# Two stacked transformer blocks on one core: attention weights loaded head by head, and four FP4 nibbles unpacked in each 16-bit word

## The chip, the core and the metric

The kernel runs on one core of a Trainium2 chip. The metric is device time in microseconds of one execution; each figure of a kernel is the median over several executions. Five engines work side by side and wait for one another through semaphores: PE (the matrix engine), VectorE (DVE in the rows), ScalarE (ACT), GpSimd (POOL) and SyncE (SP), which issues most of the DMA transfers.

## What is computed

Four stages in a row act on x of shape 2 x 512 x 256, each followed by a normalised sum with what went in:

```python
# stage 0: causal attention, 16 heads of 128, with rotary embedding
x = layernorm(h) * ln_g + ln_b
q, k, v = (x @ w.T + b for each);  q, k = rope(q), rope(k)
attn = softmax(mask(q k^T / sqrt(128)));  out = (attn v) @ wo.T + bo + h
# stage 1: MLP 256 -> 2048 -> 256, weights in FP4
low = W_packed & 15;  high = W_packed >> 4 & 15
W = LUT[interleave(low, high)] * scales (one for each block of 32)
out = (gelu(x @ Wg.T) * (x @ Wu.T)) @ Wd.T
# stage 2: linear attention with running sums, 16 heads of 16 (W_qkv, W_out)
# stage 3: MLP 256 -> 688 -> 256, weights by index into a table of 16
```

The packed codes come as int32, one byte of value (0 to 31) in each. All matrix products are made in float16 with a correction: each fp32 operand is split into a high float16 part (`h`) and a low one (`l` = value - h), and three products are added (`product`).

## The kernel before

Tokens are in 8 tiles of 128 rows, four per batch. The order of work on each engine is written out by hand, and nothing is reordered. Attention runs over 32 units (batch b, head h; `UNITS`), in steps `s` from -2 to 33. In step s PE makes the scores of unit s (`scores`), the projection of q and k of unit s+2 in two halves (`project(s + 2, 0)`, `project(s + 2, 1)`, both through the one `proj_bank`), v of unit s (`project_v`), the output projection of unit s-2 (`out_project`) and the weighted sum of unit s-1 (`weigh`). VectorE takes the row maxima (`top`, L977), corrects o (`low_o`, L1013), multiplies each projection half by cosine and sine (`rotate`, L986 and L988), and makes `low_v` (L1007) and the lows of the probabilities (`low_p`, L999). GpSimd adds the rotated halves of unit s+1 (`rotate`, L494 and L495, four ops) and makes the lows of q and k (`low_qk`, L502, two ops). ScalarE makes `exp` (L650), and the high parts (`high_qk` L669, `high_v` L674, `high_p` L661, `high_o` L681). SP turns the probabilities by DMA (`turn`).

The attention weights and those of stage 2 are split on the way. They come in 18 pieces of 128 x 1024 fp32 into a ring of four slots, `stage`. Pieces 0 to 5 hold the first eight heads of wq, wk and wv less their first two heads (768 columns); then follow wo, the other eight heads, the rest of wo, and stage 2's. The first two heads of wq, wk and wv (`EARLY`) come ahead of all in three loads of 256 KB (`early32`), which ScalarE (`high_early`, L611) and VectorE (`low_early`, L916) split. `LOWS_AT` names the step of each piece: in it ScalarE makes the high part (`high_w`, L625), for GpSimd's pieces it also scales the staged values (L627), and then either GpSimd (`low_w`, L472, `ALL_POOL_W`) or VectorE (`prepare`, L936, `DVE_LOWS`: every second piece from 6 on) makes the whole low. SP's `load_w(j + 4)` waits until the low of piece j has freed its slot. GpSimd's `rotate(u)` waits for its own lows before it.

Batch 0 is normalised and turned by PE before the steps (`turn_norm0`, `turned_x0` L923, `high_xT0` L621, `low_xT0` L929). Batch 1 is turned in steps 4 and 5 (`X0_TURN_AT`), one half each, through `proj_bank`: at the step's end PE waits for VectorE's second `rotate(s + 2, 1)`, transposes four tiles (L1337), and `turned_x0` comes behind that rotation. ScalarE normalises four tiles each in steps 2, 7 and 9 (`X0_NORM_AT`). GpSimd adds a bias row to four tiles in steps 10 and 12 (`residual`, L479).

FP4: 12 pieces of 512 columns. `unpacked(j)` and `signed(j)` on VectorE make from 512 int32 words two tiles of FP8 bit patterns and their sign bits, in five ops (L962 to L971). GpSimd multiplies each by the scales (`scaled`, L521, reading one byte in four), ScalarE and VectorE split the product (`high_fp4` L719, `low_fp4` L1114). Pieces 0 to 2 are unpacked around the end of attention, pieces 3 to 11 beside the first tiles of the first of two MLP passes (`unpack_beside`); there each tile of 128 hidden values goes through gelu (L737), `product_of` (L1162), its high part (L743) and low part on GpSimd (`low_inter`, L525), and PE's `gate_up` and `down`.

Of the kernel before, what the change touches and what calls it, by code (L numbers as in the profile page):

```python
# [79 lines left out]
def sandwich(nc, x_in, wqT, wkT, wvT, woT, bqT, bkT, bvT, bo, gT, bT, ropes, w1T, packed, scales, codes, lut, out):  # L80
    with ExitStack() as ctx:
# [3 lines left out]
        def sem(name):  # L85
# [34 lines left out]
        wh = [sb(f"w{n}h", [P, 4096], F16) for n in "qkvo"]  # L120
        wl = [sb(f"w{n}l", [P, 4096], F16) for n in "qkvo"]
# [12 lines left out]
        sign = xT[:, 0, :].bitcast(I32)  # L134
# [31 lines left out]
        early32 = pT[:, :, :, :, :].rearrange("p w k i n -> p (w k i n)").bitcast(F32)[:, 0:3 * KC * EARLY].rearrange(  # L166
            "p (w c n) -> p w c n", w=3, c=KC)
# [8 lines left out]
        bits = [prob[:, 0, 2 * i:2 * i + 2, :].bitcast(I32) for i in range(NIBBLES)]  # L176
# [13 lines left out]
        fh = [w[:, :].rearrange("p (c n) -> p c n", c=NIBBLES) for w in wh[0:3]]  # L190
        fl = [w[:, :].rearrange("p (c n) -> p c n", c=NIBBLES) for w in wl[0:3]]
# [13 lines left out]
        d_bits = sem("d_bits")  # L205
        a_fh = sem("a_fh")
# [83 lines left out]
        w_dram = [w.rearrange("(c p) n -> p c n", p=P) for w in (wqT, wkT, wvT, woT)]  # L290

        def w_piece(j):

            return W_ORDER[j]

        def w_cols(j):

# [77 lines left out]
        def _(sp):  # L375
# [1321 lines left out]
```

## Time and profile before

| | us |
|---|---|
| median of 3 runs (702.53 to 702.62) | 702.58 |
| the profiled execution | 699.39 |
| its span in the profile | 697.6 |

| engine | busy us | share of the span |
|---|---|---|
| PE | 561.1 | 80% |
| VectorE | 549.6 | 79% |
| ScalarE | 399.6 | 57% |
| GpSimd | 388.6 | 56% |

The mean granted PE clock of the span is 0.93 of full. The span is what the profiler saw of one execution from the first to the last instruction; a little time lies around it. A share of busy time is a mean over stages that have different limits, so the rows below are taken by stage. In a row of the timeline stand the start, the time until its end (of all instructions merged in the row), the engine, the line of the kernel, the operation, what is written and read, the shapes and, in brackets, how long the engine was idle before and what it waited for. Names such as `turned`, `rr` or `pT` are buffers that serve several purposes in turn.

### The profile page before, as it was taken

What the parts mean: (1) busy time and instruction counts of PE and PEld (TensorE: products, weight loads), DVE (VectorE), ACT (ScalarE), POOL (GpSimd) and SP (SyncE); (2) the same over time, 40 slices, a digit from 0 to 9 for tenths busy, and PEclk for the clock granted to TensorE, in tenths of its full rate; (3) what the DMA queues carried; (4) which work ended last, traced back from release to release, by engine and by line L of the source; (5) the groups of instructions that cost most, each with busy time, mean ns of one, the idle gap of its engine ahead of it and who ended that gap; (6) DMA issues with size and microseconds to landing.
All of it is one profiled execution on the core that took longest, in us unless ns stands there. A gap on an engine that the chain in (4) does not pass through costs nothing.

```text
span 697.6 us, 10855 instructions
## 1 busy us (share of the span) xinstructions
PE 561.1 (80%) x3843; PEld 339.9 (49%) x3848; DVE 549.6 (79%) x1103; ACT 399.6 (57%) x838; POOL 388.6 (56%) x312
## 2 busy tenths in 40 slices
PE   5378788989899999999777787969964968793494
PEld 2145456565566666666543444535532634352252
DVE  6578779878789998998799999887469494667643
ACT  4578667877776687787744344355542345462141
POOL 3698866999988787778456566211442101154021
PEclk8899989999999999999989999989989899997597
DMA  7255443433335485344332130111001010000000
GB/s 257 83 129 126 105 110 81 95 77 68 52 76 74 77 179 90 66 66 75 78 101 76 62 90 1 32 39 34 1 0 46 15 32 1 0 1 0 0 31 30
DMA packets 100741, 44.58 MB, mean 64 GB/s; under 512 B 88272, under 2 KB 93520, under 8 KB 100688
## 3 DMA queue, kind: packets, MB, share of 16 engines
q1 hardware_dynamic: 99696, 43.35, 28.1%
q8 instruction: 30, 0.49, 0.3%
q10 hardware_dynamic: 992, 0.55, 0.3%
q14 instruction: 23, 0.19, 0.1%
HBM read 21.86 MB, written 1.05 MB: 33 GB/s over the span
## 4 chain that ended last, share of the span: by engine, by line
PE 39%; DVE 29%; issue 10%; ACT 9%; POOL 6%; POOLq 0%; DVEq 0%; ACTq 0%
PE bank L1325 34%; PE bank L1501 3%; DVE turned L1153 2%; DVE stage L1182 2%; DVE turned L1162 2%; DVE stats L849 2%; POOL rr L494 1%; POOL rr L495 1%; DVE xT L964 1%; DVE pT L962 1%; DVE y L863 1%; DVE pT L963 1%; DVE pT L971 1%; DVE wql L1114 1%; DVE wkl L1114 1%
## 5 line engine op out<-in xcount | busy, mean ns | idle before, releaser
L525 POOL TENSOR_TENSOR qkl<-turned,qkh 128x512 f16<-128x512 f32 (+1 forms) x44 | 57.4, 1304 | 178.3 <-ACT qkh L743 178.3
L494 POOL TENSOR_TENSOR rr<-turned 64x512 f32<-64x512 f32 x64 | 86.7, 1354 | 12.2 <-DVE turned L988 8.2
L502 POOL TENSOR_TENSOR qkl<-rr,qkh 128x512 f16<-128x512 f32 x64 | 73.8, 1158 | 29.4 <-ACT qkh L669 27.0
L743 ACT ACTIVATE qkh<-turned 128x512 f16<-128x512 f32 (+1 forms) x44 | 27.7, 629 | 108.5 <-DVE turned L1162 108.5
L650 ACT ACTIVATE bank<-bank,nmax 128x128 f32<-128x128 f32 (+3 forms) x128 | 64.1, 501 | 37.8 <-DVE nmax L977 37.3
L495 POOL TENSOR_TENSOR rr<-turned 64x512 f32<-64x512 f32 x64 | 81.9, 1279 | 3.7
L977 DVE TENSOR_REDUCE nmax<-bank 128x1 f32<-128x128 f32 (+3 forms) x128 | 58.2, 484 | 15.0 <-PE bank L1371 13.3
L1162 DVE SCALAR_TENSOR_TENSOR turned<-bank,turned 128x512 f32<-128x512 f32 (+1 forms) x44 | 30.0, 682 | 46.4 <-PE bank L1325 20.8
L999 DVE SCALAR_TENSOR_TENSOR parts<-bank,rscaled,parts 128x128 f16<-128x128 f32 (+3 forms) x128 | 65.8, 547 | 0.3 <-ACT parts L661 0.3
L1325 PE MATMUL bank<-qkh 128*128 128x128 f16 (+3 forms) x128 | 38.9, 304 | 24.7 <-issue 16.3
L661 ACT ACTIVATE parts<-bank,rscaled 128x128 f16<-128x128 f32 (+3 forms) x128 | 57.2, 529 | 1.2 <-DMA pT<-parts 0.2
L1325 PE MATMUL bank<-pT,vh 128*128 128x512 f16 (+3 forms) x256 | 56.6, 311 | 1.5 <-DVE vl L1007 1.2
L1325 PE MATMUL bank<-xTh,wkh 128*128 128x512 f16 x128 | 50.1, 391 | 5.6 <-DVE turned L988 4.4
L1325 PE MATMUL bank<-xTh,wqh 128*128 128x512 f16 x128 | 50.5, 395 | 1.5 <-DVE turned L988 1.5
L1325 PE MATMUL bank<-xTl,wqh 128*128 128x512 f16 x128 | 50.1, 392 | 0.0
L1325 PE MATMUL bank<-xTh,wql 128*128 128x512 f16 x128 | 50.0, 391 | 0.0
L669 ACT ACTIVATE qkh<-rr 128x512 f16<-128x512 f32 x64 | 40.5, 634 | 16.1 <-POOL rr L495 16.1
L1325 PE MATMUL bank<-xTl,wkh 128*128 128x512 f16 x128 | 49.8, 389 | 0.0
L1325 PE MATMUL bank<-xTh,wkl 128*128 128x512 f16 x128 | 49.7, 388 | 0.0
L1325 PE MATMUL bank<-wvh,qkh 128*128 128x256 f16 x128 | 36.3, 284 | 16.3 <-POOL qkl L525 16.3
L1325 PE MATMUL bank<-wvh,xTh 128*128 128x128 f16 x256 | 44.6, 219 | 2.2 <-DVE ol L1013 2.2
L1325 PE MATMUL bank<-wvh,xTl 128*128 128x128 f16 x256 | 44.5, 219 | 0.0
(224 smaller groups left out, 1722.4 us busy)
## 6 DMA issues: line engine op xcount, KB each, us to landing
xa<-in_codes SPq DMA_DIRECT2D x32, 128.0 KB, 2.7
stage<-in_packed SPq DMA_DIRECT2D x12, 256.0 KB, 3.1
stage<-in_scales SPq DMA_DIRECT2D x12, 256.0 KB, 3.7
stage<-in_woT SPq DMA_DIRECT2D x4, 512.0 KB, 3.5
pT<-parts SPq DMA_TRANSPOSE x128, 2.8
x<-in_x SPq DMA_DIRECT2D x2, 512.0 KB, 7.2
stage<-in_wqT SPq DMA_DIRECT2D x2, 512.0 KB, 4.2
stage<-in_wkT SPq DMA_DIRECT2D x2, 512.0 KB, 4.0
```

The lines of the kernel that those rows point to most:

```text
L494: pool.tensor_tensor(rr[low, w, :], cos_a[part], sin_b[part], ALU.subtract)
L495: pool.tensor_tensor(rr[high, w, :], cos_b[part], sin_a[part], ALU.add).then_inc(g_rot, 1)
L502: pool.tensor_tensor(qkl[:, p, w, :], rr[:, w, :], qkh[:, p, w, :], ALU.subtract).then_inc(g_qkl, 1)
L525: pool.tensor_tensor(il[n % 2][0:rows, :], inter[0:rows, n % 2, :], ih[n % 2][0:rows, :], ALU.subtract).then_inc(g_il, 1)
L650: act.activation(row, row, ACT.Exp, bias=nmax[:, p, q:q + 1], accum_out=psum_row[:, p, q:q + 1]).then_inc(a_exp, 1)
L661: act.activation(row_parts[q][:, :, 0, :], row_bank[q][:, 0:(q + 1) * P].rearrange("p (k n) -> p k n", n=P), ACT.Copy, scale=rscaled[:, p, ...
L669: act.activation(qkh[:, p, w, :], rr[:, w, :], ACT.Copy).then_inc(a_qkh, 1)
L743: act.activation(ih[n % 2][0:rows, :], inter[0:rows, n % 2, :], ACT.Copy).then_inc(a_ih, 1)
L977: dve.tensor_reduce(nmax[:, p, q:q + 1], row_bank[q][:, 0:(q + 1) * P], AX_X, ALU.max, negate=True).then_inc(d_max, 1)
L999: dve.scalar_tensor_tensor(out=row_parts[q][:, :, 1, :], in0=row_bank[q][:, 0:(q + 1) * P].rearrange("p (k n) -> p k n", n=P), scalar=rsca ...
L1162: dve.scalar_tensor_tensor(out=inter[0:rows, n % 2, :], in0=U_bank[n % 2][0:rows, :], scalar=1 / (X_SCALE * W_SCALE), in1=gel[0:rows, n % ...
L1325: last = pe.matmul(dst, l, r, start=start and i == 0, stop=stop and i == 2, skip_group_check=skip)
```

## The change

- Weights by head. The host packs q, k, v and o of each head side by side; a piece is now one head (256 columns each of q, k, v, o), 16 pieces and two for stage 2. The early loads and their splits are gone. One piece falls in each step from -1 to 14, piece 1 in step -2, and piece 0 before the steps.
- Lows shared. Of each head's piece GpSimd makes the low of the first 768 columns, VectorE that of the last 256 (`POOL_COLS`); piece 0 is wholly VectorE's, stage 2's two are GpSimd's. ScalarE makes the highs one step ahead.
- Batch 1's transposes in mid-step. PE makes them after `project_v`, waiting for the first rotation half only; VectorE's `turned_x0` stands ahead of `low_p`.
- FP4. ScalarE copies each int32 piece to bytes (`to_bytes`); VectorE works on 256 uint16 words, each holding two bytes, so four nibbles.

```diff
-LOWS_AT = {-2: (0, 1, 2, 3), -1: (4, 5), 0: (6,), 1: (7,), ... 9: (15,), 11: (16,), 13: (17,)}
-DVE_LOWS = (6, 8, 10, 12, 14, 16)
+W_PIECES = HEADS + 2
+LOWS_AT = {-2: (1,), **{s: (s + 3,) for s in range(-1, HEADS - 1)}}
+POOL_COLS = 3 * D
+BYTES_AT = tuple(range(UNITS - 6, UNITS - 2))
...
+byte = xT[:, 0, :].bitcast(U8).rearrange("p (i n) -> p i n", n=Q_COLS)
-bits = [prob[:, 0, 2 * i:2 * i + 2, :].bitcast(I32) for i in range(NIBBLES)]
+bits = [prob[:, 0, i, :].bitcast(U8).rearrange("p (e n) -> p e n", n=Q_COLS) for i in range(NIBBLES)]
...
+def of_head(h, w, c=0):
+    o = w * D + c * DK
+    n = D if w == 3 else DK
+    return [a[:, h, o:o + n] for a in (w_all_h, w_all_l)]
 def lows_before(j):
-    g = sum(i in ALL_POOL_W for i in range(j))
-    return j - g, g
+    return min(j, HEADS), max(j - 1, 0)
... SP
-for w in range(3):
-    sp.dma_start(early32[:, w, :, :], w_dram[w][:, :, 0:EARLY]).then_inc(s_early[w], 16)
 def load_w(j):
     if j >= 4:
         by_dve, by_pool = lows_before(j - 3)
+        if by_pool:
+            sp.wait_ge(g_wl, by_pool)
+        sp.wait_ge(d_wl, by_dve)
+    src = per_head[j] if j < HEADS else w1_dram[:, j - HEADS, :]
+    sp.dma_start(stage[:, j % 4, :], src).then_inc(s_w[j % 4], 16)
... GpSimd
 def low_w(j):
     pool.wait_ge(a_wh, j + 1)
+    n = POOL_COLS if j < HEADS else W_COLS
+    pool.tensor_tensor(w_low(j)[:, 0:n], stage[:, j % 4, 0:n], w_high(j)[:, 0:n], ALU.subtract).then_inc(g_wl, 1)
-code = bits[j % 2][:, c, :].bitcast(FP8).rearrange("p (n e) -> p n e", e=4)[:, :, 0]
+code = bits[j % 2][:, c, :].bitcast(FP8)
... ScalarE
 def high_w(j):
     act.wait_ge(s_w[j % 4], 16 * (j // 4 + 1))
+    n = POOL_COLS if 0 < j < HEADS else W_COLS
+    for cols in (slice(0, n), slice(n, W_COLS))[:1 if n == W_COLS else 2]:
+        last = act.activation(w_high(j)[:, cols], stage[:, j % 4, cols], ACT.Copy, scale=W_SCALE)
+    if j:
+        last = act.activation(stage[:, j % 4, 0:n], stage[:, j % 4, 0:n], ACT.Copy, scale=W_SCALE)
     last.then_inc(a_wh, 1)
 in step(s):
-    for j in LOWS_AT.get(s, ()):
-        if j >= 2:
-            high_w(j)
+    for j in LOWS_AT.get(s + 1, ()):
+        high_w(j)
+def to_bytes(j):
+    act.wait_ge(s_raw[j % 4], 32 * (j // 4 + 1))
+    if j >= 4:
+        act.wait_ge(d_bits, 2 * (j - 3))
+    act.activation(byte[:, j % 4, :], raw[:, j % 4, :], ACT.Copy).then_inc(a_byte, 1)
+# called behind steps 26 to 29 for pieces 0 to 3, and one MLP tile ahead of unpacked(j) for 4 to 11
... VectorE
+def low_w(j):
+    cols = slice(POOL_COLS if j else 0, W_COLS)
+    dve.wait_ge(a_wh, j + 1)
+    dve.scalar_tensor_tensor(out=w_low(j)[:, cols], in0=stage[:, j % 4, cols], scalar=W_SCALE,
+                             in1=w_high(j)[:, cols], op0=ALU.mult, op1=ALU.subtract).then_inc(d_wl, 1)
 def prepare(s):          # last in step(s), behind rotate(s + 2, 1)
     for j in LOWS_AT.get(s, ()):
+        if j < HEADS:
+            low_w(j)
 def unpacked(j):
-    dve.tensor_scalar(low, r, 2, 0x1C, ALU.logical_shift_left, ALU.bitwise_and)
-    dve.tensor_scalar(high, r, 2, 0x1C, ALU.logical_shift_right, ALU.bitwise_and)
-    dve.tensor_scalar(sign, r, 4, 0x80, ALU.logical_shift_left, ALU.bitwise_and).then_inc(d_bits, 1)
+    r = byte[:, j % 4, :].bitcast(U16)
+    low, high, sign = (bits[j % 2][:, i, :].bitcast(U16) for i in range(3))
+    dve.wait_ge(a_byte, j + 1)
+    dve.tensor_scalar(low, r, 2, 0x1C1C, ALU.logical_shift_left, ALU.bitwise_and)
+    dve.tensor_scalar(sign, r, 4, 0x8080, ALU.logical_shift_left, ALU.bitwise_and)
+    dve.tensor_scalar(high, r, 2, 0x1C1C, ALU.logical_shift_right, ALU.bitwise_and).then_inc(d_bits, 1)
 in step(s):
     if there(s):
         inverse(s)
         low_v(s)
+    if s in X0_TURN_AT:
+        turned_x0(1, (X0_TURN_AT[s],))
+    if there(s):
         for q in range(TPB):
             low_p(s, q)
     if there(s + 2):
         rotate(s + 2, 1)
-    if s in X0_TURN_AT:
-        turned_x0(1, (X0_TURN_AT[s],))
... PE, in step(s)
     if there(s):
         project_v(s)
+    if s in X0_TURN_AT:
+        pe.wait_ge(d_rope, 2 * (s + 2) + 1)
+        turn_norm0(1, (X0_TURN_AT[s],))
...
     if there(s + 2):
         project(s + 2, 1)
-    if s in X0_TURN_AT:
-        pe.wait_ge(d_rope, 2 * (s + 2) + 2)
-        turn_norm0(1, (X0_TURN_AT[s],))
```

## Rows read from the trace of the kernel before

**Rows 1.** Busy time by stage: PE, PEld, DVE, ACT, POOL; granted clock; DMA share, GB/s.

```profile
34.00:202.00 168.00, 145.48 (x1195) 95.61 (x1196) 135.50 (x249) 126.41 (x305) 145.15 (x113) 0.97 0.44 92
202.00:346.00 144.00, 137.20 (x1184) 93.03 (x1184) 127.76 (x258) 110.39 (x284) 111.25 (x90) 1.00 0.50 88
346.00:435.00 89.00, 66.40 (x355) 36.96 (x355) 88.38 (x134) 37.41 (x60) 52.44 (x36) 0.90 0.23 67
```

**Rows 2.** Timeline of the opening, all engines: start, us.

```profile
6.79 0.61 ACT L611 ACTIVATE wqh<-pT 128x512 f16<-128x512 f32 x1
...
8.43 0.69 DVE L916 SCALAR_TENSOR_TENSOR wql<-pT,wqh 128x512 f16<-128x512 f32 x1
...
10.94 0.84 ACT L625 ACTIVATE wqh<-stage 128x768 f16<-128x768 f32 x1 [0.97 <-DMA stage<-in_wqT]
...
12.42 1.13 ACT L621 ACTIVATE xTh<-xT 128x512 f16<-128x512 f32 x2
...
13.07 2.31 DVE L929 TENSOR_TENSOR xTl<-xT,xTh 128x512 f16<-128x512 f32 x2 [1.40 <-ACT xTh L621]
...
15.44 1.03 PE L1463 MATMUL bank<-zerob,identb 128*128 128x512 bf16 x2 [4.91 <-DVE xTl L929]
...
19.16 0.75 DVE L986 SCALAR_TENSOR_TENSOR turned<-bank,bias_q,rope 128x512 f32<-128x512 f32 x1
...
23.71 2.47 DVE L910 SCALAR_TENSOR_TENSOR shift<-mv,rstd 128x4 f32<-128x4 f32 x3
```

**Rows 3.** Timeline, two of GpSimd and the first scores on PE.

```profile
22.92 3.24 POOL L472 TENSOR_TENSOR wkl<-stage,wkh 128x768 f16<-128x768 f32 x2 [6.04 <-ACT stage L627]
...
34.04 0.26 PE L1325 MATMUL bank<-qkh 128*128 128x128 f16 x1 [5.01 <-POOL qkl L502]
...
37.26 1.26 POOL L494 TENSOR_TENSOR rr<-turned 64x512 f32<-64x512 f32 x1 [0.17 <-POOL wvl L472]
```

**Rows 4.** Timeline of GpSimd in the steps, and the scores of unit 16.

```profile
45.09 2.17 POOL L494 TENSOR_TENSOR rr<-turned 64x512 f32<-64x512 f32 x1 [0.22 <-DVE turned L988]
...
54.65 2.13 POOL L472 TENSOR_TENSOR wol<-stage,woh 128x1024 f16<-128x1024 f32 x1 [0.73 <-ACT stage L627]
...
76.94 1.27 POOL L494 TENSOR_TENSOR rr<-turned 64x512 f32<-64x512 f32 x1 [0.17 <-POOL wql L472]
...
82.27 2.27 POOL L502 TENSOR_TENSOR qkl<-rr,qkh 128x512 f16<-128x512 f32 x2
...
151.76 2.78 POOL L479 TENSOR_TENSOR xa<-xa,bo_row 128x256 f32<-128x256 f32 x4
...
192.55 1.26 POOL L494 TENSOR_TENSOR rr<-turned 64x512 f32<-64x512 f32 x1 [0.22 <-DVE turned L988]
...
201.48 0.22 PE L1325 MATMUL bank<-qkh 128*128 128x128 f16 x1 [0.17 <-issue]
```

**Rows 5.** Timeline of VectorE's weight lows and of batch 1's first transposes.

```profile
44.93 1.22 DVE L936 SCALAR_TENSOR_TENSOR wol<-stage,woh 128x1024 f16<-128x1024 f32 x1
...
84.74 1.12 PE L1337 MATMUL bank<-identf,nrm 128*128 128x128 f32 x4 [3.47 <-DVE turned L988]
...
86.62 1.80 DVE L936 SCALAR_TENSOR_TENSOR wkl<-stage,wkh 128x1024 f16<-128x1024 f32 x1
```

**Rows 6.** VectorE's busy time in stretches that hold one unpacking each.

```profile
358.97:361.30 2.33, 2.30 (x7) 0.56 0.54 171
...
370.15:375.22 5.07, 5.04 (x6) 0.95 0.27 73
...
390.30:393.47 3.17, 3.14 (x6) 1.00 0.02 5
...
sum 44.94, DVE 44.53; mean DVE 3.71
```

**Rows 7.** One op of an unpacking (timeline), and four f16 ops (chain).

```profile
391.42 1.52 DVE L970 TENSOR_TENSOR pT<-pT,xT 128x512 int32<-128x512 int32 x1
...
450.08 1.05 DVE rope L1153 x4
```

More of the change, by code:

```diff
@@ L13 @@
 I32 = mybir.dt.int32
+U16 = mybir.dt.uint16
+U8 = mybir.dt.uint8
 P = 128
@@ L77, with sandwich @@
 TURNS = ((0, 0), (0, 1), (1, 0), (1, 1), (2, 0), (3, 0), (2, 1), (3, 1))
-def sandwich(nc, x_in, wqT, wkT, wvT, woT, bqT, bkT, bvT, bo, gT, bT, ropes, w1T, packed, scales, codes, lut, out):
+def sandwich(nc, x_in, per_head, bqT, bkT, bvT, bo, gT, bT, ropes, w1T, packed, scales, codes, lut, out):
     with ExitStack() as ctx:
@@ L488, in rotate @@
                     pool.wait_ge(g_qkl, 2 * u)
-                pieces = [j for k in range(-2, u - 1) for j in LOWS_AT.get(k, ()) if j in ALL_POOL_W]
+                pieces = [j for k in range(-2, u - 1) for j in LOWS_AT.get(k, ())]
                 pool.wait_ge(g_wl, len(pieces))
@@ L508, in step @@
                 for j in LOWS_AT.get(s, ()):
-                    if j in ALL_POOL_W:
-                        low_w(j)
+                    low_w(j)
                 if s in RESIDUAL_STEPS:
@@ L635, in _ @@
             std0_of(0, 0, eps_twice, 1.0 + LN_EPS)
-            for w in range(3):
-                high_early(w)
             high_w(0)
@@ L763, in _ @@
                 step(s)
+                if s in BYTES_AT:
+                    to_bytes(BYTES_AT.index(s))
                 if s == UNITS:
@@ L807, in _ @@
                     high_fp4(unpack_beside(m - 1))
+                if unpack_beside(m + 1) in range(4, Q_PIECES):
+                    to_bytes(unpack_beside(m + 1))
                 if m == 13:
@@ L912, in other_norms @@
                 last.then_inc(d_rstd0, 1)
-            def low_early(w):
-                dve.wait_ge(a_early, w + 1)
-                dve.scalar_tensor_tensor(out=early_cols(wl[w]), in0=early32[:, w, :, :], scalar=W_SCALE, in1=early_cols(wh[w]),
-                                         op0=ALU.mult, op1=ALU.subtract).then_inc(d_early, 1)
             def turned_x0(b, cs=range(KC)):
@@ L930, in low_xT0 @@
                                       ALU.subtract).then_inc(d_xTl, 1)
+            def low_w(j):
[3 more added lines that the diff above has]
+                                         in1=w_high(j)[:, cols], op0=ALU.mult, op1=ALU.subtract).then_inc(d_wl, 1)
             def prepare(s):
                 for j in LOWS_AT.get(s, ()):
-                    if j in DVE_LOWS:
-                        dve.wait_ge(a_wh, j + 1)
-                        dve.scalar_tensor_tensor(out=w_low(j), in0=stage[:, j % 4, :], scalar=W_SCALE, in1=w_high(j),
-                                                 op0=ALU.mult, op1=ALU.subtract).then_inc(d_wl, 1)
+                    if j < HEADS:
+                        low_w(j)
             spread0(0)
             first_norm()
-            low_early(0)
-            low_early(1)
+            low_w(0)
             dve.wait_ge(s_small, 16 * 5)
@@ L949, in _ @@
             low_xT0(0)
-            low_early(2)
             spread0(1)
@@ L1661, with of_heads @@
     w_first, w_second = by_half(a["L0_attn_wq"], a["L0_attn_wk"])
+    def of_heads(w):
+        return w.T.reshape(KC, P, HEADS, DK).transpose(2, 1, 0, 3).reshape(HEADS, P, D)
+    per_head = np.concatenate([of_heads(w) for w in (w_first, w_second, a["L0_attn_wv"])]
+                              + [a["L0_attn_wo"].T.reshape(HEADS, P, D)], axis=2)
     b_first, b_second = by_half(a["L0_attn_bq"], a["L0_attn_bk"])
```

112 lines of the change are left out of this document (24 added, 88 removed).

## The prediction

> **What bounds the kernel now.** I read the busy time by stage first [rows 1]. The attention steps (34 to 346 us) are 312 of 697.6 us. From 202 to 346 us PE is busy 137.2 of 144 and sets the pace: sixteen steps in it, about 9.05 us a step with the ends. From 34 to 202 us no engine is near that, but GpSimd is busy 145.2 of 168. The stretch 346 to 435 us, in which the FP4 weights are unpacked beside the first MLP pass, has VectorE busy 88.4 of 89 and PE only 66.4. So three places can give time: the opening, the sixteen steps that still carry weights, and the unpacking.
>
> Then the engines in order of time. Opening: ScalarE reaches the copy of xT at 12.42 because `high_w(0)` stands ahead of it and waits for its load until 10.94; VectorE's two `xTl` run 13.07 to 15.38, PE starts at 15.44, and the rotation of head 0 starts on VectorE only at 19.16, behind `low_early(2)` and batch 1's statistics [rows 2]. GpSimd does four weight lows before its rotation of unit 0 and two more behind it, and starts the rotation of unit 1 at 37.26; the scores of unit 0 start at 34.04 [rows 3]. Steps: one rotation with its two `low_qk` takes GpSimd 7.60 us (76.94 to 84.54), a 1024-column low adds 2.13 and 0.17 to the next start, and in front of it GpSimd waits 0.73 for ScalarE's `high_w`, which sits in the same step [rows 4]. From the rotation of unit 1 (37.26) to that of unit 16 (192.55) the fifteen cycles take 155.3 us, 10.35 each. Then the scores follow at 201.48, 8.93 later, since PE is the bound again [rows 3, 4].
>
> **The change, part by part. Opening.** The three early loads, three highs and three lows go; piece 0 (head 0's q, k, v and o, 512 KB) comes in their place. Before, the first 256 KB of weights were read at 6.79, with no wait for the load, and piece 0 of the old order (1.1 MB in all after x) at 10.94 [rows 2]; between these I let the new piece 0 be there at 7: `high_w(0)` of 1024 columns 7.0 to 7.95, `low_w(0)` on VectorE after the first norm 8.43 to 9.56 (1.22 as a whole [rows 5], about 1.13 from start to start). That replaces two lows of 512 columns (0.69 each at most [rows 2]), so `turned_x0` starts as before. But the copies of xT have no `high_w` before them: they start near 10.9 and end near 12.1, the two `xTl` (2.31 together now, beside a GpSimd low; I take 1.2) end near 12.9, and PE starts at 13.0. Its first projection lies within the 3.7 us between 15.44 and 19.16; I take 3.0, to 16.0. The rotation on VectorE then starts at 16.0, not 19.16. The second projection and its rotation take 1.5 and 1.4 with the gaps (an estimate; 4.4 in all from 16.0 to 20.4): GpSimd can start unit 0 at 20.4, because only one low (piece 1, near 14 to 15.6) is ahead of it. It ends 7.60 later, at 28.0 [rows 4], and the scores of unit 0 start at 28.1. The low of piece 2 takes 1.64 (two in 3.24 [rows 3]), and unit 1's rotation starts at 30.0 instead of 37.26: **-7.3 us**. Bounds: VectorE's three tiny `shift0` took 2.47 beside GpSimd's lows [rows 2] and now run beside rotations; if all of unit 1's work waits for them, 2 us are lost; nothing lets the gain exceed 9.
>
> **The steps.** Each head now has its own piece, one a step from step -1 to step 14. ScalarE makes it one step ahead, so GpSimd's 0.73 wait is gone. GpSimd: 7.60 + 0.05 + 1.64 (768 columns) + 0.17 = 9.46 us a cycle. VectorE takes the last 256 columns, about 0.4 us (1.22 at 1024 columns, 0.69 at 512 [rows 2, 5], so 0.27 for each 256). Such an op and GpSimd's exclude one another: beside VectorE's 1024-column low GpSimd's `rr` took 2.17 in place of 1.27, and where VectorE came second its low took 1.80 in place of 1.22 [rows 4, 5]. I charge 0.3 a cycle, between nothing and 0.9. Fifteen cycles: 15 x 9.46 = 141.9; 13 x 0.3 = 3.9; the two W_qkv pieces are whole on GpSimd, 2 x 0.5; the two residuals (2.78 each [rows 4]) are no longer covered by idle time, 2 x 2.84 = 5.7. ScalarE has three ops a step (0.84 each for 768 columns [rows 2], 0.4 for 256) where it had two of 1024 or one; with the three normalisations on top (steps 2, 7 and 9) `oh`, the maxima and the copy of k come late, an estimated 0.5 each, 1.5; the two `low_xT0` meet GpSimd's ops, 1.0. Sum 155.0 against 155.3: **-0.3**. So the weights take as long as before, spread evenly; GpSimd, not PE, paces these steps.
>
> Batch 1's transposes: now PE waits 3.47 us for VectorE's second rotation, transposes (1.12 [rows 5]), and only then weighs; these two steps are part of the 155.3. After the change they need only the first rotation half, done before `project_v` ends; PE gets 1.1 more work, and VectorE's copy stands ahead of `low_p`. That is 10.2 us on PE, of which 9.8 is covered by GpSimd's cycle: hidden, and already inside the 155.0 (without that cover, as at PE's 9.05 pace, it would cost about 1 each). When the last low is done PE's slack is used up: scores follow the rotation by 7.7, not 8.93: **-1.2**. The loads wait for both lows on SP, ahead of the next `turn`; they are released at the start of the next step, 6 us before SP's transposes can go, so nothing waits.
>
> **FP4.** Twelve unpackings take 44.94 us of VectorE; one with GpSimd idle 2.33; those that meet GpSimd up to 5.07 [rows 6]. The words go from 512 int32 to 256 uint16. No row has uint16. A 512-column f16 op of one input takes 0.26 (four in 1.05 [rows 7]); its half would be 0.13, and with a fixed part I take 0.20 for each of three. A two-input op on 512 columns takes 0.69 and the next starts after 0.60; less 0.27 for 256 columns it is 0.33. An unpacking: 3 x 0.20 + 2 x 0.33 + 0.05 = 1.3 to 1.4 instead of 2.33. If shifts of 16-bit words run no faster per word than the two-input ops, 1.7. Before the MLP loop all is a chain on VectorE: 0.95 + 0.8 + 0.95 = **-2.7**. In the loop the waits for GpSimd stay: an op queued behind `low_inter` or `scaled` still waits for its end (391.42: 1.52 instead of 0.69 [rows 7]). Nine lie in the loop: three of the kind of 5.07 lose 0.95, the six others, of which 390.30 is one, 0.6 (one op's wait stays). **-6.4**; bounds -2 (GpSimd's `scaled` and `low_inter` set the tile) and -11 (all the width and the waits behind it). ScalarE's twelve `to_bytes`, 0.6 each, cost nothing: four lie in steps 26 to 29, where ScalarE works 110.4 of 144 us, eight where it works 37.4 of 89 [rows 1]; uncovered they would be 7. GpSimd's fp8 input is now packed; I leave its price, for want of a row of such a form, between no change and 0.1 less an op.
>
> A rule on the first of these prices: the Trainium skill, "VectorE: DVE Perf Modes", section on the TRN2 errata, gives (58 + columns / mode) cycles at 0.96 GHz, and its tier table lets 16-bit tensor_tensor run in twice mode. By it that op would take 0.19, not 0.33, an estimate that would make the forecast 683. No row here has such an op.
>
> Sum: -7.3 - 0.3 - 1.2 - 2.7 - 6.4 = -17.9. The profiled execution took 699.39 us with a span of 697.6, so 1.8 lie around the span; the median of the runs shown is 702.58, 0.5% more. I take the difference over whole from the median: **684.7 us**.
>
> **Rivals.** (1) The unpacking stays tied to GpSimd: each piece saves 0.2 in the loop. For it: nearly every op of the 5.07 kind ends when a GpSimd op does [rows 6]. Against it: the kind of 390.30 has one wait alone. Then 684.7 + 5 = 690. (2) The shared accesses stretch every cycle by 0.9, as they did in the steps with a VectorE low [rows 4]: 13 x 0.6 = 8 more, with late maxima 12: 697. (3) Slower: VectorE's `low_w` stands in its queue ahead of the maxima of the next unit, and at that moment GpSimd has just begun its own 1.64 us low. VectorE waits it out, 1.64 + 0.33, the maxima start 2 us late, and the rotation for the unit after next follows them. If that loop carries the delay, a cycle is 11.4 and fifteen cost 24 more than before: 684.7 + 24.5 = 709. Against it: in a GpSimd-paced loop VectorE's second rotation is wanted only some 1.8 us later than it comes. It decides from 10.96 a cycle on ((155.3 + 17.6 - 8.5) / 15), the other gains being 17.6. The Trainium skill, "SBUF — State Buffer", states that the pair of ports is locked for a whole instruction and the loser fully blocks; by it this wait is the full 1.64, as 1.80 and 2.17 above suggest. (4) More: GpSimd's ops never meet VectorE's and the opening gives 9: 676.
>
> **How the numbers follow.** Likeliest 0.62; rival 1 0.14; rival 2 0.12; rival 3 0.05; rival 4 0.07. Range 676 to 697: it takes in all but rival 3 and the tails of 2 and 4. About 0.2% (1.4 us) is what this kernel's measurement can tell from no change. Faster 0.90, same 0.03, slower 0.07 (rival 3, and rival 1 and 2 together with a poor opening).
>
> **What would show it.** Right: first GpSimd rotation near 20, second near 30; scores of units 0 to 15 spaced 9.5 to 10, the two steps with transposes no longer than the others by more than 1; GpSimd idle under 0.5 us a step there; scores of unit 16 near 192.5; the three unpackings before the loop 1.4 each; the loop's first product 11.5 us earlier than now and its first twelve tiles 6 us shorter. Wrong: piece 0 landing after 8.5 us; cycles above 10.5; 16-bit words at 0.34 or more an op; a tile that still ends with VectorE waiting for GpSimd.

## The result and the profile after

The changed kernel takes 677.40 us (median of 4 runs, 675.08 to 679.59) beside 702.56 for the kernel before in the same runs: ratio 0.9664, 95% interval 0.9642 to 0.9686. The forecast was 684.7 in a range of 676 to 697, so the sign and the range were right and the size was not: 25 us came where 17.9 were forecast. The profiled execution took 677.76 us with a span of 676.0, so the spans differ by 21.6. The other 3.5 us are there because the profiled execution of before (699.39) was 3.2 faster than its median and that of the changed kernel 0.4 slower. What is explained below are the 21.6.

Three stages of the changed kernel, in the view of busy time by stage (columns as in [rows 1]): the steps that carry weights, the attention steps behind them, and the unpacking.

```profile
34.00:187.00 153.00, 131.15 (x1107) 86.25 (x1106) 137.38 (x239) 125.24 (x306) 139.38 (x112) 1.00 0.48 102
187.00:340.60 153.60, 144.80 (x1252) 98.26 (x1251) 134.49 (x271) 118.14 (x301) 118.87 (x97) 1.00 0.47 85
340.60:411.50 70.90, 57.84 (x354) 33.39 (x352) 67.79 (x132) 40.98 (x68) 46.14 (x36) 1.00 0.28 84
```

In the last row VectorE is still the bound (67.8 of 70.9), but the stretch is 17.5 us shorter. Its granted clock is 1.00 where it was 0.90 [rows 1]. In the first row VectorE and GpSimd are both busy about 90% of the time.

The opening, in the timeline of all engines (columns as in [rows 2]):

```profile
6.67 1.04 ACT L588 ACTIVATE w_all_h<-stage 128x1024 f16<-128x1024 f32 x1
...
8.32 1.22 DVE L900 SCALAR_TENSOR_TENSOR w_all_l<-stage,w_all_h 128x1024 f16<-128x1024 f32 x1
...
15.57 0.75 DVE L953 SCALAR_TENSOR_TENSOR turned<-bank,bias_q,rope 128x512 f32<-128x512 f32 x1
...
20.03 1.25 POOL L460 TENSOR_TENSOR rr<-turned 64x512 f32<-64x512 f32 x1 [3.78 <-DVE turned L955]
...
21.38 1.51 DVE L900 SCALAR_TENSOR_TENSOR w_all_l<-stage,w_all_h 128x256 f16<-128x256 f32 x1
...
23.03 0.59 PE L1293 MATMUL bank<-xTh,w_all_h 128*128 128x512 f16 x1 [4.53 <-DVE w_all_l L900]
...
29.79 0.31 PE L1293 MATMUL bank<-qkh 128*128 128x128 f16 x1
...
31.52 1.37 POOL L460 TENSOR_TENSOR rr<-turned 64x512 f32<-64x512 f32 x1 [2.25 <-DVE turned L955]
```

Piece 0 is there when ScalarE wants it, VectorE's first rotation starts at 15.57 (16.0 forecast) and GpSimd's at 20.03 (20.4 forecast). The next line was in no sum: VectorE's part of head 1's low stands behind both rotation halves and the tiny `shift0` ops, and PE waits 4.53 us for it.

PE comes out of this wait slower. One of its 512-column matmuls takes 0.38 us at 17.26 and 0.63 at 23.41, and the view of busy time shows the granted clock at 0.50, which is the lower level (1.2 GHz):

```profile
23.00:30.00 7.00, 5.46 (x14) 1.84 (x15) 1.41 (x2) 2.66 (x5) 6.13 (x5) 0.50 0.22 75
```

So both projection halves of head 1 run at half speed, and GpSimd waits 2.25 us for VectorE's rotation behind them.

The steps, in the timelines of GpSimd, VectorE and PE:

```profile
58.88 1.65 POOL L438 TENSOR_TENSOR w_all_l<-stage,w_all_h 128x768 f16<-128x768 f32 x1
60.70 1.26 POOL L460 TENSOR_TENSOR rr<-turned 64x512 f32<-64x512 f32 x1 [0.17 <-POOL w_all_l L438]
...
142.66 2.96 POOL L445 TENSOR_TENSOR xa<-xa,bo_row 128x256 f32<-128x256 f32 x4
...
187.39 1.26 POOL L460 TENSOR_TENSOR rr<-turned 64x512 f32<-64x512 f32 x1 [0.17 <-POOL w1l L438]
```

```profile
59.19 1.62 DVE L900 SCALAR_TENSOR_TENSOR w_all_l<-stage,w_all_h 128x256 f16<-128x256 f32 x1
60.73 0.61 DVE L944 TENSOR_REDUCE nmax<-bank 128x1 f32<-128x128 f32 x2
...
98.78 1.90 DVE L894 TENSOR_TENSOR xTl<-xT,xTh 128x512 f16<-128x512 f32 x1
100.60 1.48 DVE L900 SCALAR_TENSOR_TENSOR w_all_l<-stage,w_all_h 128x256 f16<-128x256 f32 x1
```

```profile
74.81 0.66 PE L1305 MATMUL bank<-identf,nrm 128*128 128x128 f32 x4 [0.68 <-DVE turned L955]
...
84.58 0.66 PE L1305 MATMUL bank<-identf,nrm 128*128 128x128 f32 x4 [0.16 <-DVE turned L955]
...
195.08 0.22 PE L1293 MATMUL bank<-qkh 128*128 128x128 f16 x1 [0.97 <-issue]
```

VectorE's 256 columns last 1.62 us here, not 0.4 (over steps 0 to 12 they last 1.04 to 1.82; at 31.36, where VectorE comes first, 0.41). The op starts 0.31 us behind GpSimd's low and ends 0.28 us behind it, and the maxima stand behind it: this is rival 3's mechanism, at a lower price. The transposes wait 0.68 and 0.16 us where they waited 3.47 [rows 5].

The unpackings, in the view of VectorE's busy time in twelve stretches as in [rows 6]; the first, fifth, seventh and last of them and the sum:

```profile
341.17:342.25 1.08, 1.05 (x6) 1.00 0.19 37
...
359.80:363.38 3.58, 3.55 (x7) 1.00 0.12 43
...
376.53:377.61 1.08, 1.05 (x6) 1.00 0.06 15
...
402.87:405.33 2.46, 2.43 (x7) 1.00 0.00 0
sum 26.77, DVE 26.36; mean DVE 2.20
```

The one at 376.53 in VectorE's timeline, and what GpSimd did then. It is the same piece as that of 390.30 in [rows 6, 7]:

```profile
376.53 0.22 DVE L928 TENSOR_SCALAR pT<-xT 128x256 uint16<-128x256 uint16 x1
...
377.06 0.29 DVE L937 TENSOR_TENSOR pT<-pT 128x256 uint16<-128x256 uint16 x1
377.26 0.42 DVE L938 SCALAR_TENSOR_TENSOR pT<-xT,pT 128x256 uint16<-128x256 uint16 x1
```

```profile
377.36 1.34 POOL L490 TENSOR_TENSOR qkl<-turned,qkh 128x512 f16<-128x512 f32 x1 [4.28 <-ACT qkh L709]
378.66 2.15 POOL L486 TENSOR_TENSOR rr<-pT,stage 128x512 f32<-128x512 fp8e4 x2
```

Before, `low_inter` began while the third op (390.97) ran, and the fourth waited it out (1.52 [rows 7]), in GpSimd's timeline of before:

```profile
391.13 1.27 POOL L525 TENSOR_TENSOR qkl<-turned,qkh 128x512 f16<-128x512 f32 x1 [4.28 <-ACT qkh L743]
```

Now all five ops have started when it begins, and it is GpSimd that waits a little (1.34 us, beside 1.15 for the `low_inter` at 380.78).

Where the 21.6 us come from, by the starts of the same instructions in both traces: the scores of unit 16 start at 195.08, not 201.48 [rows 4] (-6.4). One step, that of unit 22, is 1.0 longer. From the scores of unit 31 to the twelfth `product_of` behind the first ("product 12" below) it is 17.5 us less, 77.2 for 94.8: 3.8 up to the first product (355.4 for 364.5), 13.8 in the twelve tiles. The two ends of that stretch, before and then after, in the timelines of PE and VectorE:

```profile
339.62 0.22 PE L1325 MATMUL bank<-qkh 128*128 128x128 f16 x1 [1.17 <-issue]
...
434.39 0.68 DVE L1162 SCALAR_TENSOR_TENSOR turned<-bank,turned 128x512 f32<-128x512 f32 x1
```

```profile
334.30 0.22 PE L1293 MATMUL bank<-qkh 128*128 128x128 f16 x1 [0.63 <-issue]
...
411.53 0.68 DVE L1130 SCALAR_TENSOR_TENSOR turned<-bank,turned 128x512 f32<-128x512 f32 x1
```

Behind that, in tiles that the change does not touch, 1.2 us are lost (264.4 for 263.2). That is no sign of a cause: in the traces of the runs below this stretch takes 260.9 to 264.4 us, with the same work in it.

### The profile page after: what moved, and what is told of

It is laid out like the page before. It is cut to its first block, busy times and chain, and to the rows that moved or that the text cites. A ratio compares the mean times of both kernels' runs of the same rounds, so it can differ in the third digit from the quotient of the medians.

```text
span 676.0 us, 10925 instructions
## 1 busy us (share of the span) xinstructions
PE 552.0 (82%) x3848; PEld 336.5 (50%) x3848; DVE 537.8 (80%) x1110; ACT 408.7 (60%) x867; POOL 383.0 (57%) x317
## 4 chain that ended last, share of the span: by engine, by line
PE 38%; DVE 29%; issue 10%; ACT 9%; POOL 8%; DMA 3%; SPq 2%; POOLq 0%; DVEq 0%; ACTq 0%
PE bank L1293 33%; DVE turned L1121 3%; PE bank L1453 2%; DVE stage L1150 2%; DVE parts L966 2%; DMA pT<-parts 2%; DVE turned L1130 2%; DVE w_all_l L1082 2%; DMA x<-in_x 2%; POOL rr L461 2%; DVE stats L819 1%; POOL rr L460 1%; POOL qkl L468 1%; SPq L377 1%; POOL qkl L490 1%
## 5 line engine op out<-in xcount | busy, mean ns | idle before, releaser
L1293 PE MATMUL bank<-xTh,w_all_h 128*128 128x512 f16 (+1 forms) x304 | 117.9, 388 | 12.7 <-DVE w_all_l L900 7.7
L1293 PE MATMUL bank<-xTl,w_all_h 128*128 128x512 f16 (+1 forms) x304 | 118.0, 388 | 0.0
L1293 PE MATMUL bank<-xTh,w_all_l 128*128 128x512 f16 (+1 forms) x304 | 117.9, 388 | 0.0
L460 POOL TENSOR_TENSOR rr<-turned 64x512 f32<-64x512 f32 x64 | 82.3, 1286 | 17.2 <-DVE turned L955 12.2
L461 POOL TENSOR_TENSOR rr<-turned 64x512 f32<-64x512 f32 x64 | 81.1, 1266 | 3.7
L1293 PEld LDWEIGHTS bank<-xTh,w_all_h 128*128 128x128 f16 (+1 forms) x304 | 30.2, 99 | 47.0 <-issue 15.2
L1293 PEld LDWEIGHTS bank<-xTh,w_all_l 128*128 128x128 f16 (+1 forms) x304 | 30.3, 100 | 37.6 <-issue 3.0
L1293 PE MATMUL bank<-w_all_h,xTh 128*128 128x128 f16 x256 | 44.6, 219 | 0.8 <-DVE ol L980 0.8
L1293 PE MATMUL bank<-w_all_l,xTh 128*128 128x128 f16 x256 | 44.5, 219 | 0.0
L1293 PE MATMUL bank<-w_all_h,xTl 128*128 128x128 f16 x256 | 44.5, 219 | 0.0
L1293 PE MATMUL bank<-w_all_h,qkh 128*128 128x256 f16 x128 | 36.4, 284 | 9.1 <-POOL qkl L490 9.1
```

Source lines behind the costliest of these rows:

```text
L460: pool.tensor_tensor(rr[low, w, :], cos_a[part], sin_b[part], ALU.subtract)
L461: pool.tensor_tensor(rr[high, w, :], cos_b[part], sin_a[part], ALU.add).then_inc(g_rot, 1)
L1293: last = pe.matmul(dst, l, r, start=start and i == 0, stop=stop and i == 2, skip_group_check=skip)
```

## The experiments

Each is timed against the kernel before on its own chip (medians of before 700.4 to 701.6). Executions of one kernel differ by up to 5.6 us. The opening is the same in the changed kernel, e2 to e5, e8 and e11, and yet the scores of unit 2 start between 48.2 and 51.3 in their traces; the tail behind product 12 differs too, as said. The changed kernel's ratio (0.9642 to 0.9686) overlaps those of e2, e4, e5, e10 and e11, so these five can't be told from it by time alone, and for small effects I read the spacing of like instructions in the traces, one of each kernel.

**e1: the FP4 part alone.** The kernel before with the diff's FP4 lines and nothing else of it:

```diff
+    act.activation(byte[:, j % 4, :], raw[:, j % 4, :], ACT.Copy).then_inc(a_byte, 1)
-    dve.tensor_scalar(low, r, 2, 0x1C, ...)      # 512 int32 words
+    dve.tensor_scalar(low, r, 2, 0x1C1C, ...)    # 256 uint16 words
-    code = bits[j % 2][:, c, :].bitcast(FP8).rearrange("p (n e) -> p n e", e=4)[:, :, 0]
+    code = bits[j % 2][:, c, :].bitcast(FP8)
```

> The kernel before with the FP4 part alone: bytes made by ScalarE, 256 words of 16 bits, packed codes for GpSimd; weights and transposes as before. Theory A: the FP4 part is worth what the trace of the changed kernel shows between the end of attention and product 12 (17.5 us: 3.7 before the MLP loop, 13.8 in it), whatever the weights do: 702.6 - 17.5 = 685, and within 683.5 to 687. Rival B: the forecast term of 9.1 us was right for the unpacking alone, and the rest of the gain in the loop came with the other parts (the loop entered earlier, other buffers): 693 to 694.

Measured: 685.05 us, ratio 0.9772 (0.9740 to 0.9804), 15.4 us less than before on the same chip. From the scores of unit 31 to product 12 this kernel takes 77.3 us; the changed one takes 77.2, the one before 94.8. Theory A holds: the FP4 part is 17.5 us there, with the old weights too. The whole shows less because the scores of unit 16 start at 203.7 in this execution, 2.3 later than before's. It also lost 0.8 in the step of unit 22, with the old weights and the old loads, so that loss is none of the weight part's.

**e2: transposes last again.** The changed kernel with PE's transposes and `turned_x0` at the end of steps 4 and 5:

```diff
-    pe.wait_ge(d_rope, 2 * (s + 2) + 1)     # ahead of out_project
-    turn_norm0(1, (X0_TURN_AT[s],))
...
+    pe.wait_ge(d_rope, 2 * (s + 2) + 2)     # behind weigh(s - 1)
+    turn_norm0(1, (X0_TURN_AT[s],))
```

> The changed kernel with batch 1's transposes back at the end of steps 4 and 5, as before; all else as in the changed kernel. Theory A: the move is worth what steps 4 and 5 show, 14.4 + 13.15 us before against 10.4 + 9.8 after, less what the two steps would now be spared, since GpSimd, which sets the pace here, stands still meanwhile and can't catch up: plus 4 to 7 us, 681 to 685. Rival B (the forecast's reading, a cost that is hidden either way): GpSimd's cycle covers the wait: plus 0 to 1.5, 677 to 679.

Measured: 678.90 us, ratio 0.9671 (0.9634 to 0.9709). From the scores of unit 3 to those of unit 8 it takes 53.4 us in place of 50.9. So the place is worth 2.5 us, and nothing of it is taken back later. Theory A asked too much and B too little. Steps 4 and 5 take 27.5 us before, 21.5 here and 20.2 in the changed kernel: 6.0 of what they shrank by belongs to the new order of the weights and 1.3 to the place of the transposes, whose other 1.2 lies in step 6.

**e3: words of 8 bits.**

```diff
-    r = byte[:, j % 4, :].bitcast(U16)
-    dve.tensor_scalar(low, r, 2, 0x1C1C, ALU.logical_shift_left, ALU.bitwise_and)
+    r = byte[:, j % 4, :].bitcast(U8)       # 512 words, and so the other four ops
+    dve.tensor_scalar(low, r, 2, 0x1C, ALU.logical_shift_left, ALU.bitwise_and)
```

> The changed kernel with VectorE's five ops on 512 words of 8 bits in place of 256 of 16 bits; the bytes, the packed layout and GpSimd's part stay. Theory A: the halved number of words on VectorE is what pays. The unstalled unpacking goes from 1.08 back to about 2.0 (five ops near 0.4), and on a stretch that VectorE sets twelve of them cost 8 to 11 us: 686 to 688. Rival B: the packed codes that GpSimd reads and the shorter collisions with it are what pays, and VectorE's own width is covered by them: no more than 3 us, 677 to 680.

Measured: 690.53 us, ratio 0.9847 (0.9816 to 0.9879). In the stretch to product 12 this kernel loses 14.2 us, more than theory A's 8 to 11. Its first unpacking, in VectorE's timeline, alone on the two engines:

```profile
340.62 0.43 DVE L928 TENSOR_SCALAR pT<-xT 128x512 uint8<-128x512 uint8 x1
...
341.75 0.69 DVE L937 TENSOR_TENSOR pT<-pT 128x512 uint8<-128x512 uint8 x1
342.36 0.68 DVE L938 SCALAR_TENSOR_TENSOR pT<-xT,pT 128x512 uint8<-128x512 uint8 x1
```

These are the durations that the int32 ops of before have in the same view where nothing holds them up (0.42, 0.69 and 0.68). A byte is no cheaper than a word of 32 bits, and twelve unpackings take 43.9 us in place of 27.1 (45.9 before, the last op's end included).

**e4: GpSimd reads every fourth byte.**

```diff
-    code = bits[j % 2][:, c, :].bitcast(FP8)
+    code = prob[:, 0, j % 2, :].bitcast(FP8).rearrange("p (n e) -> p n e", e=4)[:, :, 0]
```

> The changed kernel with GpSimd reading every fourth byte of a tile of 2048 (it reads the tile's own low, high and sign bytes and zeros in place of the codes, so the FP4 weights are wrong; the amount of work is that of the kernel before on GpSimd and that of the changed one on VectorE; two small memsets are added). Theory A: VectorE's words pay, GpSimd's layout little: its pair of ops goes from 2.15 to 2.70 us, 0.55 a piece, of which at most half of the nine in the loop shows: plus 0 to 3 us, 677 to 680. Rival B: the packed codes pay: plus 6 us or more, above 683.

Measured: 677.83 us, ratio 0.9652 (0.9613 to 0.9691). Theory A: the stretch to product 12 is 2.6 us longer. (GpSimd multiplies sign bytes and zeros in place of the codes, so its FP4 weights are not the real ones; two small memsets on VectorE are added.) GpSimd's timeline has the same piece as above:

```profile
382.12 2.49 POOL L486 TENSOR_TENSOR rr<-pT,stage 128x512 f32<-128x512 fp8e4 x2
```

The pair takes 2.49 us spread and 2.15 packed; over all pieces one op takes 0.17 to 0.19 more (means of 1.57 and 1.48 us for the two buffers, beside 1.38 and 1.31). With e3 the 17.5 us are accounted for but for 0.7: about 14.2 by the 16-bit words, 2.6 by the packed codes. No run separates the granted clock, which rose too (0.90 to 1.00). But nothing is left for it to explain: VectorE, which sets this stretch, spends 18.8 us less on the twelve unpackings, more than the stretch gives back.

**e5: words of 32 bits.**

```diff
-    r = byte[:, j % 4, :].bitcast(U16)
-    dve.tensor_scalar(low, r, 2, 0x1C1C, ALU.logical_shift_left, ALU.bitwise_and)
+    r = byte[:, j % 4, :].bitcast(U32)      # 128 words, and so the other four ops
+    dve.tensor_scalar(low, r, 2, 0x1C1C1C1C, ALU.logical_shift_left, ALU.bitwise_and)
```

> The changed kernel with VectorE's five FP4 ops on 128 words of 32 bits (eight nibbles a word) in place of 256 of 16 bits. Theory A (price by the number of words, whatever their width): five ops near 0.15 to 0.2 us, an unpacking near 0.8 in place of 1.08, and since the run with 8-bit words moved this stretch by 14 us for 256 words more an op, 128 words less give up to another 4 us where VectorE still sets the tile: 672 to 676. Rival B: with four tile intervals already set by PE and gelu, VectorE's ops are no longer the bound: within 1 us of 677.4.

Measured: 675.49 us, ratio 0.9629 (0.9600 to 0.9657); 1.2 us less in the stretch. Its timeline says why no more:

```profile
341.60 0.23 DVE L929 TENSOR_SCALAR pT<-xT 128x128 uint32<-128x128 uint32 x1
...
342.13 0.29 DVE L938 TENSOR_TENSOR pT<-pT 128x128 uint32<-128x128 uint32 x1
342.35 0.28 DVE L939 SCALAR_TENSOR_TENSOR pT<-xT,pT 128x128 uint32<-128x128 uint32 x1
```

Only the last op gains (0.28 for 0.42). The price is not one by the number of words alone, as theory A had it.

**e6: low split 512 to 512.**

```diff
-POOL_COLS = 3 * D
+POOL_COLS = 2 * D
```

> The changed kernel with the low of a head's piece split 512 to 512 columns between GpSimd and VectorE, not 768 to 256. Theory A (forecast: GpSimd's own work paces the steps that carry weights): its low costs 0.54 less in each, fourteen steps give 5 to 7.5 us, the rotation of unit 16 near 181 in place of 187.4: 670 to 672. Theory B (what the trace of the changed kernel suggests: VectorE's low waits for the end of GpSimd's low, 1.62 to 1.82 us for work of 0.4, and stands ahead of the maxima): GpSimd's low ends 0.54 earlier, VectorE's own part is 0.3 longer, so VectorE's op lasts about 1.4 and a cycle shrinks by only 0.2 to 0.3, some 3 to 4 us in all: 673 to 675. If the collision is worth nothing and VectorE sets the pace by its own work: slower by 4, 681.

Measured: 673.96 us, ratio 0.9616 (0.9595 to 0.9638). The plain steps take 9.40 us, not 9.62; from the rotation of unit 2 to that of unit 16 it is 2.0 us less. That is B's sign and a little under its size, and not the 5 to 7.5 of a kernel that only GpSimd paces: VectorE's op still lasts 1.41, and GpSimd's first `rr` now lasts 1.50 for 1.26. The two halves start together here too, and this split gives its 2.0 us all the same.

**e7: VectorE's low in mid-step.**

```diff
     inverse(s)
+    prepare(s)
     low_v(s)
...
     rotate(s + 2, 1)
-    prepare(s)
```

> The changed kernel with VectorE's low of 256 columns moved from the end of a step (where it starts with GpSimd's low and waits it out) to the place ahead of low_v, where VectorE idles 0.44 us for ScalarE; head 1's low also moves ahead of the second rotation half of head 0. Theory A (rival 3's mechanism is in the changed kernel at a smaller price: VectorE's queue carries the wait of 1.2 us into the maxima): VectorE's op meets an rr op of 1.27 at a random point, lasts about 1.0, and 0.44 of it is covered, so VectorE's chain is about 1 us shorter a step; GpSimd then sets it at 9.46 plus 0.2 to 0.4 for being delayed itself: 9.37 to 9.6 stays, gain 0 to 3 us, and the steps of 10.4 and 11.3 shrink: 673 to 677; the product of head 1 starts 1.5 us earlier. Rival B: GpSimd is the only bound and now loses 0.4 a step to VectorE's op: plus 3 to 6, 680 to 683.

Measured: 672.66 us, ratio 0.9589 (0.9549 to 0.9629). VectorE's op, in its timeline:

```profile
56.19 1.12 DVE L900 SCALAR_TENSOR_TENSOR w_all_l<-stage,w_all_h 128x256 f16<-128x256 f32 x1
```

It lasts 1.12, and the plain step 9.47: GpSimd's own 9.46, as forecast. The two steps of 11.29 fall to 9.88 and 10.39, because the weight low of 1.48 us no longer stands behind `low_xT0` there; `low_xT0` itself still lasts 1.89 beside GpSimd's low. In all it is 2.4 us less from the rotation of unit 2 to that of unit 16. The opening gains nothing: the scores of unit 2 start at 51.4, 2.0 later than in the changed kernel. Another 2.5 us of the lower time lie behind product 12, where nothing was changed.

**e8: batch 1's residual late.**

```diff
-RESIDUAL_STEPS = {10: 0, 12: 1}
-X0_NORM_AT = {2: (1, "nrm"), 7: (0, "xa"), 9: (1, "xa")}
+RESIDUAL_STEPS = {10: 1, 17: 2, 18: 3, 19: 4, 20: 5}      # one tile each from step 17 on
+X0_NORM_AT = {2: (1, "nrm"), 7: (0, "xa"), 16: (1, "xa")}
```

> The changed kernel with batch 1's residual taken out of the weight steps: its normalisation on ScalarE in step 16 and not 9, its four bias adds on GpSimd one each in steps 17 to 20 and not together in step 12, where GpSimd has 1.4 us of slack a step. Theory A: the step after step 12 falls from 12.28 to 9.6 us, and what was hidden before is paid by no one: minus 2.7, 674.7. Rival B: the steps from 17 on take it back, 0.7 an add: no change, 677. The normalisation moved from step 9 gives nothing by either (step 9 takes 9.6 now).

Measured: 670.89 us, ratio 0.9570 (0.9553 to 0.9588). The step of unit 13 falls from 12.28 to 9.62 and the later steps take nothing back: theory A. The step of unit 10 falls from 10.38 to 9.63 as well, which I had not expected: the normalisation of step 9 was on ScalarE's path. The rest of the 6.5 us to the changed kernel's median lies in the opening, which is the same (1.2), and in the spread of the runs.

**e9: the gains together**: e5, e6, e7 and e8, and

```diff
     prepare(s)
+    if s - 4 in X0_TURN_AT:
+        low_xT0(1, (X0_TURN_AT[s - 4],))
     low_v(s)
...
-    if s - 2 in X0_TURN_AT:
-        low_xT0(1, (X0_TURN_AT[s - 2],))
```

> The changed kernel with what gave time in the runs so far: the low split 512 to 512, VectorE's part ahead of low_v, batch 1's residual late (as in e8), words of 32 bits; and batch 1's low_xT0 also ahead of low_v, two steps later. Theory A (waits on VectorE's queue, GpSimd's work and PE's own 9.05 a step are three near bounds, and the first two now fall under the third): fourteen steps lose 0.3 to 0.5 each (4 to 6 us), the two of 11.3 another 3, the residual 2.7, the words 1.2: 677.4 - 11 to 13 = 664.5 to 666.5. Rival B: the gains overlap, since each of them freed the same bound: the step stays at 9.4, and only residual, words and one of the others count: 670 to 671.

Measured: 668.33 us (5 runs), ratio 0.9533 (0.9518 to 0.9547), the fastest version here, 9 us under the changed kernel. The plain steps take 9.24. From the scores of unit 2 to those of unit 16 it is 7.1 us less, so the result stands between the two theories. VectorE's 512 columns last 0.90 us. In this kernel PE does not wait for head 1's low in the opening, and the scores of unit 0 start at 28.1, the forecast's number. Yet those of unit 2 start where they did (49.5 for 49.4). In the view by stage the changed kernel comes first here, then e9:

```profile
28.00:39.00 11.00, 9.12 (x57) 4.97 (x55) 7.67 (x16) 6.11 (x17) 7.81 (x7) 0.81 0.16 55
39.00:50.00 11.00, 8.42 (x72) 5.33 (x73) 10.43 (x18) 9.28 (x23) 10.56 (x9) 1.00 0.53 120
```

```profile
28.00:39.00 11.00, 7.99 (x56) 4.44 (x57) 7.86 (x15) 7.51 (x19) 9.21 (x8) 0.84 0.21 62
39.00:50.00 11.00, 9.70 (x71) 5.70 (x69) 8.02 (x17) 7.82 (x21) 9.20 (x8) 0.84 0.48 114
```

The granted clock is 0.84 in both stretches in e9, and 1.00 in the second one of the changed kernel: part of each is at the lower level (1.2 GHz), behind the 2.8 to 3.7 us in which PE stood waiting for q and k. The steps of units 0 and 1 take 10.7 each and use up what the earlier start gave. They take 10.7 each in e7 and e10 too, and 9.3 each in e8, where the granted clock is 1.00 from 28 to 50.

**e10: all the low on GpSimd.**

```diff
-POOL_COLS = 3 * D
+POOL_COLS = 4 * D      # and VectorE's low_w(j) for j > 0 left out
```

> The changed kernel with every head's low (but head 0's) whole on GpSimd, 1024 columns, and none on VectorE. Theory A (the rows so far: GpSimd 9.46 a cycle with 768 columns, VectorE's chain 9.6 with its stalled low): GpSimd's cycle becomes 9.95 and sets the pace alone, the steps of 9.37 to 9.6 become 9.95, those of 10.4 and 11.3 shrink since VectorE meets nothing at the step's end: plus 2 to 5, 679.5 to 682.5. Rival B (the stall on VectorE costs more than the columns that it spares GpSimd): no change or faster, 674 to 677.5.

Measured: 676.45 us, ratio 0.9640 (0.9625 to 0.9654). Theory A is refuted. The plain step does take 9.86 (9.95 expected), but the two of 11.29 fall to 10.4 and 10.5, and from the scores of unit 2 to those of unit 16 it takes 145.6 us beside 145.7. The share that VectorE takes is worth nothing as the changed kernel places it: what GpSimd is spared, VectorE waits.

**e11: each copy to bytes twice.**

```diff
+    act.activation(second[:, j % 4, :], raw[:, j % 4, :], ACT.Copy)
```

> The changed kernel with ScalarE's to_bytes issued twice, the first time into an unused tile: twelve more ops of about 0.6 us, four in steps 26 to 29 and eight beside the first MLP pass. Theory A (forecast: ScalarE has room at both places): no change, 676 to 678.5. Rival B (ScalarE is on the path there): plus 0.6 each, up to 7: 680 to 684.

Measured: 676.52 us, ratio 0.9645 (0.9626 to 0.9665); the stretch from product 0 to product 12 takes 56.3 us for 56.1. Of the four steps with a copy only that of unit 28 is longer (9.65 for 9.12). So ScalarE's bytes cost next to nothing at both places.

## Why the prediction was right, and where its size was off

**Opening: -7.3 forecast, -5.7 measured** (unit 1's rotation at 31.52, not 30.0). Up to the first rotation every step was right to 0.7 us; PE began 0.5 late (13.54), and its first projection, put at 3.0, took 2.0. What failed was "only one low (piece 1, near 14 to 15.6) is ahead of it": that is GpSimd's share alone. VectorE's share of piece 1 lies behind both rotation halves of unit 0, PE waits 4.53 us for it, and then runs at the lower clock; the sum has neither. e7 and e9 take the wait away. In e9 the rotation of unit 1 starts at 29.2, in e7 only at 31.6, with a granted clock of 0.53 from 14 to 18 us and 0.69 from 18 to 23.

**Steps: -0.3 forecast, +0.6 measured.** From 31.52 to 187.39 the fifteen cycles take 155.9 us (155.0 forecast). Its base was right: GpSimd's plain 9.46 is there, as e7's 9.47 shows. The contention charged at 0.3 a cycle shows as 0.15, the difference between 9.62 and e7's step, so 2 us in place of 3.9. The residual was right at 2.7 a step (e8). Mis-sized was `low_xT0`: 1.0 forecast for two, 3.3 in the steps of 11.29 beside 9.62; e7 took back 2.3 of it. That the sum came out within 1 us is in part luck, since the two errors cancel. The sign given for it, scores of units 0 to 15 "spaced 9.5 to 10", did not come: they are 9.1 to 12.3 apart, 10.33 in the mean. **Scores behind the rotation: -1.2 forecast and measured** (7.69 for 8.93).

**Transposes:** forecast as hidden and worth nothing of their own. Their price at the step's end is 2.5 us (e2), so the move was worth something, inside a sum that came out right.

**FP4: the term that was mis-sized, -9.1 forecast, -17.5 measured.** Two steps of its working failed. First the price of an op: 0.20 from start to start for the three shifts and 0.33 for the two others. The shifts are at 0.14, the `tensor_tensor` op at 0.20, and only the `scalar_tensor_tensor` op at 0.33. An unpacking takes 1.08, not 1.35, and the piece saves 1.25, not 0.95. The Trainium skill's rule in "VectorE: DVE Perf Modes", in its tier table, that 16-bit `tensor_tensor` runs in twice mode is borne out by this: 256 words of 16 bits take 0.29, as long as 128 words of 32 bits (e5). The second failed step was "the waits for GpSimd stay". Of the nine pieces in the loop (each with its last op's end) the three of 5.16 us save 1.4 to 2.1, the three of 3.84 save 1.4, that of 3.37 saves 1.3, and the two of 3.25, of which 390.30 is one, save 2.1: there all five short ops have started before `low_inter` begins, and the wait is gone. Together the nine save 14.7 us of VectorE's time where 6.4 were forecast, and the twelve tiles 13.8. That is outside the bound of -11 given for "all the width and the waits behind it", which was taken from the too high price. The layout that GpSimd reads, left at "between no change and 0.1 less", was 0.17 to 0.19 less an op, and 2.6 us in all (e4).

**What was hidden** stayed hidden: the bytes (e11), SP's waits. **Rivals.** Rival 1, that the unpacking stays tied to GpSimd and each piece saves 0.2, is wrong: the nine save 1.3 to 2.1 each, though seven of them still wait for GpSimd (2.1 to 3.8 us in all for a piece that takes 1.15 alone). Rival 3's mechanism is there in every step that carries weights (1.04 to 1.82 us for 0.4), but the cycle is 9.6 in a plain step and 10.39 in the mean, below its deciding 10.96; taking the wait out of VectorE's queue (e7) shortens a plain step by 0.15 only. The Trainium skill's "SBUF — State Buffer", section "Who interferes with whom", says that the loser waits for the whole instruction; the op that ends 0.28 behind GpSimd's agrees. Rival 2 (0.9 a cycle) is wrong: one op waits, and a plain step shows 0.15 of it. Rival 4 has the nearest number, 676 for the measured 677.4, but by luck: neither of its conditions holds, for the opening gave 5.7, not 9, and the ops of GpSimd and VectorE still meet. The time lies near that end of the range because the FP4 term was too small.

The remaining step, 1.0 at unit 22, is not the weight part's (e1). There 2 MB of FP4 loads are in flight, and PE waits 1.06 us for a transposed tile. Over the thirteen traces the step grows, roughly, with the slowest landing of the four transposes issued just before: 6.3 us and a step of 9.75 before, 8.0 and 10.75 in the changed kernel, 8.7 and 11.29 in e4. Why they land later I did not settle; of the kernel before there is one trace only.

## What to carry to other kernels

When a queue is full of short ops that meet another engine's, price a faster op twice: by its own width, and by the waits that it escapes because the whole group now fits ahead of the other engine's next op. Splitting an op between two engines that exclude one another gives little if both halves start together: nothing for 768 and 256 columns (e10), 2 us for 512 and 512 (e6). What pays is to put one half where its queue idles anyway (e7, e9). And for each piece of work shared by two engines, look up who waits for the later half before the first use.

## What the runs showed of the hardware

VectorE's bitwise ops, alone, last 0.42 (shift and mask), 0.69 (two tensors) and 0.68 us (`scalar_tensor_tensor`) on 512 words of 8 bits, 0.22, 0.29 and 0.42 on 256 words of 16 bits, and 0.22, 0.29 and 0.28 on 128 words of 32 bits. All nine lie within 0.02 us of (151 + words / mode) / 0.96 GHz, where the mode is the number of words handled in a cycle, with modes 2, 1, 1, then 4, 2, 1, then 2, 1, 1. So a shift handles words of 16 bits at twice the rate of the other widths, an op of two tensors does too, and `scalar_tensor_tensor` gains nothing from any width. The Trainium skill gives this form for fp32 `tensor_tensor` in "VectorE: DVE Perf Modes", section on the TRN2 errata, and its (58 + columns / mode), from which the forecast's 0.19 came, is nearer to the time from start to start (0.20 measured). GpSimd's multiplication of 512 FP8 codes by fp32 scales takes 1.08 us with packed codes and 1.25 with one byte in four (halves of the pairs above).
